# First quad's maxima from float32 projections without a stack; norms, head scalings, value copies and casts of the first batches moved to GpSimd and ScalarE; the whole order of steps written anew

## What is computed

```python
xn = _layernorm(x, axis=-1)
x = x + _L0_attn_ref(xn, ...) + _L0_ffn_ref(xn, ...)      # causal attention; block: causal attention + 8 experts
xn = _layernorm(x, axis=-1)
x = x + _L1_attn_ref(xn, ...) + _L1_ffn_ref(xn, ...)      # full attention; 8 experts, top 2
```

## Time and profile before

| what | us |
|---|---|
| median of 3 runs | 717.04 (716.78 to 718.7) |
| the profiled execution, its own time | 717.42 |
| its span, first to last instruction | 715.7 |
| PE busy in the span | 688.1 |
| DVE / ACT / POOL busy | 564.3 / 522.7 / 192.7 |

### The profile page before, as it was taken

How to read it: one execution, slowest core, us unless ns; L and a number is a source line. 1 busy time by engine, 2 the same in 40 slices (tenths; PEclk the granted TensorE clock), 3 DMA queues, 4 the chain that set the end, 5 groups by cost and what they waited for, 6 DMA issues and landing times.

```text
span 715.7 us, 27610 instructions
## 1 busy us (share of the span) xinstructions
PE 688.1 (96%) x12078; PEld 346.0 (48%) x12078; DVE 564.3 (79%) x1089; ACT 522.7 (73%) x645; POOL 192.7 (27%) x457
## 2 busy tenths in 40 slices
PE   6589999999999999999999999999999999999996
PEld 2243444575644545446444355366554646533234
DVE  6689998365799987778999787687886676899966
ACT  6278877855677757777787968767889767688892
POOL 5255545212341211212444000212453001110000
PEclk9569999999999999999999999999999999999999
DMA  5453514010130211030133100220122000030011
GB/s 137 120 145 96 162 41 115 19 64 21 29 93 2 56 43 46 18 101 24 35 105 93 40 19 7 70 57 18 30 75 77 3 4 19 23 90 15 13 41 41
DMA packets 42150, 39.52 MB, mean 55 GB/s; under 512 B 14360, under 2 KB 37328, under 8 KB 41808
## 3 DMA queue, kind: packets, MB, share of 16 engines
q1 hardware_dynamic: 40688, 36.20, 17.9%
q10 hardware_dynamic: 1152, 1.05, 0.6%
q0 software_dynamic: 192, 0.52, 0.2%
HBM read 10.47 MB, written 1.44 MB: 17 GB/s over the span
## 4 chain that ended last, share of the span: by engine, by line
PE 83%; DVE 9%; ACT 3%; issue 2%; DMA 1%; POOL 1%; ACTq 0%; SPq 0%; DVEq 0%; POOLq 0%
PE psum L865 45%; PE psum L964 16%; PE psum L943 9%; PE psum L916 9%; DVE neg_max L558 4%; ACT probs L811 2%; PE psum L921 2%; DVE acc L713 2%; PE psum L881 1%; DMA q_stack<-part 1%; DMA heads_raw<-head_sums 0%; DVE normed_y L468 0%; POOL rstd L1076 0%; DVE normed_x L468 0%; DVE stats L445 0%
## 5 line engine op out<-in xcount | busy, mean ns | idle before, releaser
L558 DVE TENSOR_REDUCE neg_max<-psum 128x2 f32<-128x1024 f32 (+2 forms) x320 | 345.4, 1112 | 76.3 <-PE psum L921 46.9
L811 ACT ACTIVATE probs<-psum 128x1024 f32<-128x1024 f32 (+1 forms) x320 | 288.1, 938 | 96.6 <-PE psum L943 95.1
L964 PE MATMUL psum<-probs,v_ones 128*32 128x512 f32 (+3 forms) x1536 | 158.4, 496 | 0.1
L835 ACT ACTIVATE probs<-psum,col 128x512 f32<-128x512 f32 x160 | 100.2, 685 | 55.5 <-PE psum L865 55.2
L1115 POOL TENSOR_SCALAR_AFFINE_SELECT probs<-probs 128x512 f32<-128x512 f32 x128 | 81.4, 640 | 189.2 <-ACT probs L811 186.7
L865 PE MATMUL psum<-ew,probs 128*32 128x128 f32 x4096 | 124.9, 274 | 0.0
L916 PE MATMUL psum<-k_stack,q_stack 64*128 64x512 bf16 (+3 forms) x768 | 115.3, 336 | 8.0 <-DMA q_stack<-part 4.4
L865 PEld LDWEIGHTS psum<-ew,probs 128*32 128x32 f32 x4096 | 109.5, 110 | 18.1 <-issue 15.3
L865 PE MATMUL psum<-normed_T_a,ew 128*32 128x512 f32 x1024 | 117.7, 593 | 0.0
L943 PE MATMUL psum<-q_stack,k_stack 64*128 64x512 bf16 (+3 forms) x768 | 110.8, 330 | 4.0 <-DVE neg_max L558 2.2
L753 ACT ACT_TABLE_LOAD x70 | 89.8, 1283 | 1.2
(11 more groups left out here) (134 smaller groups left out, 474.0 us busy)
## 6 DMA issues: line engine op xcount, KB each, us to landing
q_stack<-part SPq DMA_DIRECT2D x66, 128.0 KB, 2.5
k_stack<-part SPq DMA_DIRECT2D x66, 128.0 KB, 2.5
heads_raw<-head_sums SPq DMA_DIRECT2D x24, 128.0 KB
heads_inv<-inverses SPq DMA_DIRECT2D x12, 256.0 KB, 3.3
ew<-w_expert_in SPq DMA_DIRECT2D x4, 512.0 KB, 4.6
ew<-w_expert_out SPq DMA_DIRECT2D x4, 512.0 KB, 5.3
q_stack<-k_stack SPq DMA_DIRECT2D x14, 128.0 KB, 2.5
q_stack<-maxT SPq DMA_DIRECT2D x48, 32.0 KB, 1.9
```

What stands on the lines that cost most here:

```text
L558: eng.tensor_reduce(neg_max[:, q % 2, :, xs[0]:xs[-1] + 1, i], src, AX_X, ALU.max, negate=True).then_inc(vector_done.sem, 1)
L811: eng.activation(dst, src, ACT.Exp, scale=SCALE).then_inc(probs_ready.sem, 1)
L835: ins = eng.activation(probs[:, order.slot[step[:-1]], 2 * k + f, :], two_banks(step)[:, f, :], ACT.Gelu_apprx_tanh if layer else ACT.Gelu ...
L964: ins = eng.matmul(sum_bank[32 * c:32 * c + V_COLS, q0:TILES * P], v_ones[u][:, j, g // 2 * QH + c, col0:col0 + V_COLS], probs[:, order.sl ...
```

## The change

It has these parts:

1. **First quad without a stack.** New steps `("first", 0, 0)` and `("first", 0, 1)` project queries and keys of the first four heads alone, from weights that ScalarE has sorted into `proj_first` (in `head_sums`, zeroed by VectorE). VectorE copies the queries twice, each time times a column of `head_of_row` (0 or 1 for each row), so that each copy keeps one head of each half; ScalarE copies the keys. The first quad's `max` matmuls (now L1025) multiply these in float32, on halves of 64 rows, and wait for no stack. The wait for the stack moves to whatever reads it first (`stack_landed`). All later quads are unchanged.
2. **Norms.** `NORM_BY_GPSIMD`: h of sequence 0, x and h of sequence 1 are normalized by GpSimd (four operations each); `rstd` of x and of h become two instructions of 128x4.
3. **Head scalings.** `HEADS_BY_GPSIMD`: `headsT` of the first three attentions is multiplied by GpSimd.
4. **ScalarE** copies the values of (0,0), (1,0) and (0,2) out of PSUM (`VALUES_BY_SCALAR`), and casts the first parts of (0,0) too (`CAST_BY_SCALAR`). Its second `clear_keys` and the sorting of the other weights come later (chain C).
5. **The last attention's end.** Instead of writing the inverses to HBM and reading them back, TensorE spreads them with 32 matmuls against a constant `spread` (`heads_spread`), and VectorE multiplies from PSUM. For all attentions `heads_den` gets a semaphore of its own (`sums_landed`), so the inversion no longer waits for `heads_raw`.
6. **`SCORE` is written anew** from first to last character. The same steps stand in it, with the new ones; the loads of the experts' weights come later. ScalarE has 74 table loads in its list where it had 71.

```diff
-CAST_BY_SCALAR = ((0, 1), (1, 1), (1, 0))
+NORM_BY_GPSIMD = ((0, "h"), (1, "x"), (1, "h"))
+HEADS_BY_GPSIMD = ((0, 0), (0, 1), (1, 1))
+VALUES_BY_SCALAR = ((0, 0), (1, 0), (0, 2))
+CAST_BY_SCALAR = ((0, 0), (0, 1), (1, 1), (1, 0))
...
 SCORE = """
-AAAAAAAA6A6A0AKAAAKA1KA6A6M2M4M0M2M4M0A6M2AALM4AT6M0M2AM4KM0M2S4A6S0M4LS2M0S4AM2T6M0S4AM2VAM4KM0S2M4S2VM0S2M4KVS0M2T
...
+AAAAACAAA6A6A0A1A6AM2AAAM4M0KM2M4CM0KT6KA0M2M4M0S2A6S4CM0M2M4S0A6A2S0M4M0M2AT6VAAM4S0VAM2M4M0S2A6AS4M2S0VKT6M4KM2KS0
...
+        q_first, k_first = (heads_inv, headsT), heads_raw
+        proj_first = head_sums[:, 0, 0:2 * P].rearrange("p (k c) -> p k c", k=2)
...
+                elif kind == "first" and step[2] == 0:
+                    src = bank(step)
+                    eng.wait_ge(vector_done.sem, 1)
+                    for x in range(2):
+                        eng.tensor_scalar(q_first[x][:, :], src, head_of_row[:, x:x + 1], None, ALU.mult)\
+                           .then_inc(vector_done.sem, 1)
...
+                elif kind == "first" and step[2] == 1:
+                    eng.wait_ge(work_full.sem, order.work[step] + 1)
+                    eng.activation(k_first[:, :], one_bank(step), ACT.Copy).then_inc(scalar_done.sem, 1)
...
-                            ins = eng.matmul(dst[:, a, col0:col0 + keys],
-                                             q_stack[slot][rows_of, head, i * P:(i + 1) * P],
-                                             k_stack[slot][rows_of, head, 0:keys], start=True, stop=not CAUSAL[u])
+                            queries = q_stack[slot][rows_of, head, :] if q else q_first[x][rows_of, :]
+                            seen = k_stack[slot][rows_of, head, 0:keys] if q else k_first[rows_of, 0:keys]
+                            ins = eng.matmul(dst[:, a, col0:col0 + keys], queries[:, i * P:(i + 1) * P], seen,
+                                             start=True, stop=not CAUSAL[u])
...
+                elif kind == "heads_spread":
+                    eng.wait_ge(vector_done.sem, order.dve["heads_inverse", *step[1:]])
+                    eng.wait_ge(spread_made.sem, 1)
+                    dst = bank(step)
+                    for n in range(HD):
+                        for c in range(COLUMN_TILES):
+                            some = slice(COLUMN * c, COLUMN * c + COLUMN)
+                            ins = eng.matmul(dst[some, HALF * n:HALF * n + HALF], spread[:, n, some], heads_den[:, :],
+                                             start=True, stop=True)
...
+            def normalize(b, what):
+
+                if what == "x":
+                    eng.wait_ge(x_loaded, 16 * (b + 1))
+                if b > 0:
+                    eng.wait_ge(vector_done.sem, order.dve["turn", b - 1, what])
+                eng.wait_ge(gpsimd_done.sem, order.pool["norm", b, what])
+                for t in range(TILES):
+                    eng.tensor_scalar(normed[what][:, t, :], x_in[:, t, :], mean_var_of[0][:, t, 0:1],
+                                      rstd_of[0][:, int(what == "h"), t:t + 1], ALU.subtract, ALU.mult)\
+                       .then_inc(gpsimd_done.sem, 1)
```

More of the change, by code:

```diff
@@ L63, in chains @@
         front += [("stats", b, "x"), ("norm", b, "x")] + ([("masks", b)] if b == 0 else [])
[L64 removed]
+        front += [("turn", b, "x")] + ([("first", b, 0), ("first", b, 1)] if b == 0 else []) + [("project", b, 0, 0), ("project", b, 0, 1), ("second", b, 0, 0),
                   ("second", b, 0, 1), ("parts", b, 0), ("norm", b, "h"), ("project", b, 0, 2),
@@ L386, in part_made, with normed_at, heads_at @@
             return gpsimd_done.sem, order.pool["parts", b, u] - 1 + side
+        def normed_at(b, what):
+            if (b, what) in NORM_BY_GPSIMD:
+                return gpsimd_done.sem, order.pool["normed", b, what]
+            return vector_done.sem, order.dve["norm", b, what]
+        def heads_at(b, u):
+            if (b, u) in HEADS_BY_GPSIMD:
+                return gpsimd_done.sem, order.pool["heads_norm", b, u]
+            return vector_done.sem, order.dve["heads_norm", b, u]
         def fill_piece(eng, step, side):
@@ L442, in _ @@
                         eng.wait_ge(x_loaded, 16 * (b + 1))
+                        for other in "xh":
+                            if b > 0 and (b - 1, other) in NORM_BY_GPSIMD:
+                                eng.wait_ge(*normed_at(b - 1, other))
                     after_writer({"x": "var_eps0", "a": "a_sum", "y": f"acc{b % 2}"}[what], f"var_eps{n_set}")
@@ L458, in _ @@
                     order.dve[step] = written[f"var_eps{n_set}"] = vector_done.count()
-                elif kind == "norm":
+                elif kind == "norm" and step[1:] not in NORM_BY_GPSIMD:
                     what = step[2]
@@ L527, in _ @@
                     order.dve[step] = n
-                elif kind == "project":
+                elif kind == "project" and step not in order.act:
                     u = step[2]
@@ L877, in _ @@
                         eng.wait_ge(made.sem, N_IDENT)
-                    eng.wait_ge(vector_done.sem, order.dve["norm", b, what])
+                    eng.wait_ge(*normed_at(b, what))
                     dst = bank(step)
@@ L881, in _ @@
                         ins = eng.transpose(dst[:, t * P:(t + 1) * P], src[:, t, :], ident[:, :])
+                    ins.then_inc(work_full.sem, 1)
+                    work_full.count()
+                elif kind == "first":
+                    k = step[2]
+                    eng.wait_ge(first_sorted.sem, 2)
+                    eng.wait_ge(vector_done.sem, order.dve["turn", b, "x"])
+                    ins = columns(bank(step), proj_first[:, k, :], normed_T["x"][:, :])
                     ins.then_inc(work_full.sem, 1)
@@ L1168, in _ @@
                     if b > 0:
-                        eng.wait_ge(vector_done.sem, max(order.dve["norm", b - 1, "x"], order.dve["norm", b - 1, "h"]))
+                        for what in "xh":
+                            eng.wait_ge(*normed_at(b - 1, what))
                         eng.wait_ge(gpsimd_done.sem, order.pool["bias", b - 1, 0])
```

223 lines of the change are left out of this document (162 added, 61 removed).

## The result

The changed kernel takes 723.39 us (median of 6 runs, 721.34 to 725.06), the kernel before 717.36 beside it (716.54 to 718.70). The ratio is 1.0073, with a 95% interval of 1.0058 to 1.0088: slower by 0.7%, where 711.2 us was forecast. The profiled execution took 722.66 us, of which 720.8 are its span.

What follows compares the result with a forecast made beforehand. The prediction took TensorE (PE) to bound the kernel, through its work, gaps and clock. Its terms, 4.2 - 5.0 + 4.8 + 1.0 + 0.8 = 5.8 us off the median of 717.04, gave 711.2 us, range 704.5 to 717.5.

Steps and rivals of the forecast that it cites:

- Term 1: Start, before the first turn of maxima: PE's gap of 8.5 us shrinks to 4.1 plus 0.2; gain 4.2 us.
- the 0.6 named as proof of an error: Sign at the start: the prediction is wrong if `normed_h` on GpSimd takes over 0.6 us each.
- Term 2: First quad: two added projections, 1.8 us, and float32 instead of bfloat16 maxima, 3.2 us; loss 5.0 us.
- Term 3: Start: half clock from about 23 us, full again at 33 to 36; PE busy 9.5 us at half clock; gain 4.8 us.
- Term 4: Up to 100 us: VectorE loses near 8 us of work, which shortens PE's gaps from 46.4 us; gain 1.0 us.
- Term 5: End of the kernel: an early inversion takes away VectorE's 2.0 us wait for `heads_raw`; gain 0.8 us.
- under 0.5 us: Sign at the end: term 5 is right if the inversion waits under 0.5 us.
- Term 6: Split `rstd`, table loads and new order in 100 to 700 us: put at 0, plus or minus 2.5 us.
- the 6 that the prediction named: Sign: the prediction is wrong if PE's gaps from 100 to 700 us are above 6 us in sum.
- GpSimd's queue: Rival, sequence 1: norms delay the cuts and PE waits at `values`, up to 3.2 us; 719.2 to 720 us, chance 0.09.
- Given back in the middle: Rival: the new order gives back between 100 and 700 us what the start wins; 717 us, chance 0.06.
- the clock never falls: Rival, start: the clock stays full or falls for a moment only; 707.5 us, chance 0.15.

Runs made afterwards that it cites:

- oldorder_first_spread: Kernel before, its order kept from the second quad on, with the float32 first quad at its start and the spread of the inverses at its end; 718.47 us, ratio 1.0009.
- before_warm: Kernel before with 36 matmuls of zeros added in PE's three gaps ahead of the first maxima; 719.15 us, ratio 1.0019 to the kernel before.
- norm_all_dve: Changed kernel with all norms moved back from GpSimd to VectorE, nothing else touched; 720.58 us, ratio 1.0041 to the kernel before.
- before_light: Kernel before, with VectorE taking the maxima of the first three quads over half of the keys only (another computation); 715.19 us, ratio 0.9959.
- oldorder_first: As oldorder_first_spread, but without the spread end: the round trip through HBM is left at the end; 718.83 us, ratio 1.0017 to the kernel before.
- reordered_start2: oldorder_first_spread with its first steps reordered and attention 1's value clearing and projection behind the first scores; 716.55 us, ratio 0.9980 to the kernel before.

## Why the prediction was wrong, step by step

The step that failed is the treatment of PE's gaps. The prediction added work, gaps and clock as if each could change without the others, and put the gaps that a change in one place opens in another at nothing. It forecast 6.0 us less of gaps, and 6.1 us more came; its terms for PE's busy time were right together.

- **Term 1, gap before the first maxima (+4.2).** VectorE was through at 21.0 (22.1). One piece was mis-sized: "the nearest is an addition of the same shape, 0.46 us". The norm, a subtraction and a multiplication with a number for each partition, took 0.785 us on GpSimd, inside the bound of 1.18 and above the 0.6 named as proof of an error. That is 1.3 us for the four tiles; the norm's start was 0.5 us later than its sum has it, and PE was through 0.6 us sooner. The gap was 6.4 us, not 4.1. Worked into the sum, the term is 1.9. In oldorder_first_spread, without this norm on GpSimd, the gap up to 24.6 us shrank by 5.6 us, and the next stretch took 4.5 of them back.
- **Term 2, added PE work (-5.0): right within 0.6.** The two added projections took 1.7 us, and the quad takes 5.6 us with its masks (25.78 less 6.44 less 13.71) where 5.0 was taken. The pairs of 512 columns come 0.94 us apart without their masks (0.88 was taken) and 1.00 with them; all eight pairs without masks sum to 5.0 us, not 4.4. The Trainium skill (FP8 and Floating Point Precision, TensorE Precision Notes) gives true FP32 four passes, and the estimate by it was 4.6 us. The trace agrees for the pairs of 512 columns, 0.94 against 4 x 0.23 = 0.92 us; the shorter ones cost more for each column.
- **Term 3, the clock (+4.8): the count right, its worth nothing.** At the half clock PE was busy 2.4 us from 25.8 to 28.2 us and 3.5 and 3.4 us near 63 and 80, together 9.3 us, where 9.5 was forecast (18.5 before). That it is the forecast's number is luck: it was to be one stretch up to 33 or 36 us, and it was three. But before_warm shows what such a gain buys where it stands alone: 4.5 us less of PE work from 24.6 to 46.4 us, and 4.5 us more of gaps. The prediction saw that VectorE was busy 19.2 of 21.8 us and then wrote "For the gaps of 24.6 to 46.4 us (3.1) I count nothing: less VectorE work shortens them, a full clock exposes VectorE". Those two were set off against each other without a number. PE's work and PE's gaps are no independent terms where another engine sets the pace; by the same token the added work of term 2 need not have cost its size. In the old order terms 1, 2, 3 and 5, 4.8 us in the forecast, came to a loss of 0.6 us (1.0009) that cannot be told from nothing.
- **Term 4, relief of VectorE (+1.0): wrong in sign.** PE's gaps from 46.4 to 100 us went from 2.8 to 7.7 us. VectorE was relieved, busy 29.7 instead of 37.4 us from 60 to 100 us, but it stood still with PE for `normed_h`. 3.7 us of PE's gaps are the wait for `normed_h`, and in norm_all_dve, without this wait, they are still 8.2 us. before_light shows what relief is worth where nothing is moved to another engine: 3 us for 7, the better clock included.
- **Term 5, the end (+0.8): half right, not seen in the time.** The inversion comes 2.7 us behind the last values (4.9 before), but its wait did not go, as was forecast ("under 0.5 us"); it moved to `heads_den` and is 3.19 us. oldorder_first_spread and oldorder_first, with and without the new end, cannot be told apart (1.0009 and 1.0017).
- **Term 6, the order (0 plus or minus 2.5): the loss was there.** The gaps from 100 to 700 us grew by 2.3 us, to 6.1, just above the 6 that the prediction named. The runs put 2.3 us on the new order too, but that the two numbers are alike says little: in norm_all_dve, which is faster, these gaps are 8.2 us. A part is named (`normed_a` and `normed_y`, slower beside GpSimd), the rest is many small gaps.
- **The rivals.** The slower one, GpSimd's queue, was given 9% and 719 to 720 us. It came, but PE stood at the turn of `normed_h`, not at the values; its 3.7 us are near the 3.2 given. It accounts for 2.3 us of the loss. "Given back in the middle", 6%, came too, in its mechanism. They were counted as exclusive; they came together, and the clock had no worth to set against them. So the result lies above every time that was named. The rival "the clock never falls" misread its row: from 14 us on the clock was full through two waits of PE of 2.2 and 1.9 us with a turn of 0.7 between, not through 3.5 us of waits and turns.

By the ratios of the runs the loss splits so: norms 0.0032 (after against norm_all_dve), new order with the scalings and two of the value copies 0.0032 (norm_all_dve against oldorder_first_spread), float32 quad and end in the old order 0.0009: together 0.0073, or 5.2 us of 717. The three add up because each starts where the other ends. The first two are just clear of zero, with intervals nearly as wide as themselves, and the third is not, so their sizes are rough. What the three value copies and two casts by ScalarE do was not tried by itself.

## What to carry to other kernels

When PE's gap and its clock at the start look like the gain, ask what the engine is that ends this stage, here VectorE with 9.98 of 10 us busy from 50 to 60 us, and when *it* can be done sooner; PE busy most of a stretch at half clock is no proof that PE sets its pace. Filling the gaps with idle work is a cheap test of that (one run), if its trace is read for whether the clock stayed and the first real work came on time. A small operation moved to a queue is priced by what stands behind it in that queue, here the split of the maxima, for which PE waits, and by what it does to VectorE beside it.

## What was not expected of the hardware

- GpSimd took 0.785 us for subtract and multiply with per-partition numbers on 128x128 float32, but 0.46 us for the addition of two tiles of that shape; VectorE 0.28 for the former where GpSimd was idle beside it (1.11 us for four).
- GpSimd's work slowed VectorE's norm: 1.11 us for four tiles alone, 1.42 with a cut beside a part of it, 1.79 with cuts, 2.75 with cuts and a scaling, 3.55 with cuts and `part` all along. This holds with either order (1.42 and 1.11 in the kernel before).
- Matmuls of zeros kept the granted clock at full (1.00 from 16 to 28 us in before_warm), where before it had fallen at 19.7 us. The time did not follow. Lighter maxima for VectorE raised it too, from 0.50 to 0.82 between 24.6 and 46.4 us.
- Kernels with the float32 quad scatter more: 716.1 to 725.6 us in the 12 runs of norm_all_dve and 713.4 to 719.4 in those of reordered_start2, while the kernel before stays within 3.3 us in 25 runs, 3.4 in 29 and 5.3 in 33. Why was not tried. One part is seen in the traces: from 10 to 14 us the clock was full in the profiled execution of the changed kernel and half in that of norm_all_dve, and the same four projections took 3.7 and 6.3 us.
